# An attention block with two feed-forward halves on one core: split-format key norms, and values made ahead in the odd head's steps

## The reference

```python
qr = q * phase; kr = k * phase                     # rotation, complex
s  = einsum('bihd,bjhd->bhij', qr, conj(kr)).real
qn = (q.real**2 + q.imag**2).sum(-1)               # query norms
kn = (k.real**2 + k.imag**2).sum(-1)               # key norms
maha   = maximum(qn + E*E*kn - 2*E*s, 0) / V       # E, V: per head and distance
logits = coef * log1p(maha / nu) - 0.5 * DH * log(V)
A   = softmax(causal(logits))
out = A @ v;  y = concat(out.real, out.imag) @ Wo
```

## Time and profile before

| | |
|---|---|
| median of 3 runs | 1696.93 us |
| span of the profiled execution | 1693.8 us |
| median less that span | 3.1 us |
| first scores of the loop | 257.64 us into the span |
| TensorE, DVE, ACT, POOL busy | 97%, 88%, 86%, 58% |

### The profile page before, as it was taken

The page is one execution under the profiler, slowest core; times in us unless marked ns, Lnnn a source line. Parts: engine busy times, 40 slices in busy tenths (PEclk is TensorE's granted clock), DMA queues, the critical chain, the costliest instruction groups (busy, mean ns, idle before and its releaser), DMA issues. The chain is left out here.

```text
span 1693.8 us, 30993 instructions
## 1 busy us (share of the span) xinstructions
PE 1642.7 (97%) x9690; PEld 1337.0 (79%) x9690; DVE 1483.9 (88%) x3380; ACT 1452.4 (86%) x2909; POOL 974.3 (58%) x826
## 2 busy tenths in 40 slices
PE   5999988999999999999999999999999999899998
PEld 4787866888888888888788888888887887777876
DVE  6878877999899989999999998999899989977665
ACT  6677678999999999999999999999999999765765
POOL 3564546566566656665655565566566656345565
PEclk9999999999999999999999999999999999999999
DMA  6000032232223322232232323232332222100000
GB/s 177 1 1 1 1 103 66 63 91 62 77 70 75 74 68 79 63 78 65 77 79 63 91 57 82 54 91 60 82 79 63 69 70 51 26 7 7 13 11 15
DMA packets 50482, 100.03 MB, mean 59 GB/s; under 512 B 8208, under 2 KB 25872, under 8 KB 50320
## 3 DMA queue, kind: packets, MB, share of 16 engines
q1 hardware_dynamic: 50320, 98.07, 22.5%
HBM read 17.95 MB, written 5.24 MB: 14 GB/s over the span
## 5 line engine op out<-in xcount | busy, mean ns | idle before, releaser
L1495 POOL TENSOR_TENSOR early<-early 128x1024 f32<-128x1024 f32 x127 | 303.2, 2387 | 470.0 <-PE pS L1183 258.6
L654 POOL TENSOR_TENSOR hid_lo_d<-hid_d,hid_hi_d 128x512 fp32r<-128x512 f32 x176 | 231.5, 1316 | 218.7 <-ACT hid_hi_d L559 212.1
L1387 ACT ACTIVATE early<-early,qnorm 128x128 f32<-128x128 f32 (+3 forms) x512 | 247.0, 554 | 68.3 <-DVE early L1578 66.4
L1183 PE MATMUL pS<-early 128*128 128x128 f32 (+3 forms) x1024 | 297.6, 433 | 0.3 <-PEq L105 0.3
L1371 ACT ACTIVATE early<-early,nmax 128x128 f32<-128x128 f32 (+3 forms) x512 | 281.6, 562 | 6.9 <-DVE nmax L1565 6.7
L1183 PEld LDWEIGHTS pS<-early 128*128 128x128 f32 x1024 | 164.7, 191 | 96.0 <-issue 61.4
L1574 DVE SCALAR_TENSOR_TENSOR pS<-pS,ek 128x1280 f32<-128x1280 f32 x128 | 191.4, 1495 | 55.3 <-PE pS L1183 54.4
L1504 POOL TENSOR_TENSOR ek<-early 128x128 f32<-128x128 f32 (+3 forms) x256 | 216.7, 881 | 3.6 <-ACT early L1379 3.0
L1504 POOL TENSOR_TENSOR ek<-decay,early 128x128 f32<-128x128 f32 (+3 forms) x256 | 215.3, 876 | 0.0
L1400 ACT ACTIVATE early<-early,params 128x512 f32<-128x512 f32 (+1 forms) x256 | 196.9, 819 | 0.0
L1198 PEld LDWEIGHTS pV<-ones,early 128*128 128x128 f32 x1016 | 134.3, 193 | 61.3 <-issue 61.3
(11 more groups left out here) (394 smaller groups left out, 3883.7 us busy)
## 6 DMA issues: line engine op xcount, KB each, us to landing
early<-early SPq DMA_DIRECT2D x263, 256.0 KB, 3.6
early<-trig_d SPq DMA_DIRECT2D x64, 64.0 KB, 2.0
trig_d<-early SPq DMA_DIRECT2D x3, 1024.0 KB, 6.9
early<-in_w SPq DMA_DIRECT2D x3, 704.0 KB, 9.0
x_sb<-in_x SPq DMA_DIRECT2D x4, 512.0 KB, 8.4
early<-in_wqk SPq DMA_DIRECT2D x16, 128.0 KB, 3.4
cos<-trig_d SPq DMA_DIRECT2D x32, 64.0 KB, 2.3
sin<-trig_d SPq DMA_DIRECT2D x32, 64.0 KB, 2.1
```

What stands on the lines that cost most here:

```text
L654: g.tensor_tensor(hid_lo[:, par], hid[:, par], hid_hi[:, par].bitcast(F32), ALU.subtract).then_inc(lo_done, 1)
L1183: last = pe.matmul(s.pS[:, span(I)], rot[:, I * P:(I + 1) * P], rot[:, N:N + (I + 1) * P], start=True, stop=True)
L1387: last = a.activation(u[:, span(I)], u[:, span(I)], ACT.Relu, bias=qnorm[:, r % 2, I:I + 1])
L1495: g.tensor_tensor(rot[:], by_cos[:], crossed[:], ALU.add).then_inc(S["rot_done"], 1)
```

## The change

Key norms. GpSimd (POOL) makes a high and a low half of the squared keys, ahead of `rotate` in each step. TensorE takes the four query-norm products first, waits for both halves, and makes the key norms as two split products with a copy of the ones in F32R. ACT may overwrite the squares when the low half is made.

Values. The batches of a pair get other steps: batches 0, 1, 2 of the next pair are made in steps 11, 13, 15 of this pair (odd head), batches 3 to 7 in steps 1, 3, 5, 7, 8 of their own pair. The first pair keeps its batches in steps 0 to 7, and the last has none in its odd head. There are four buffers for even-head values in place of three, and the waits count values as they are made.

Room in SBUF comes from a smaller scratch for dynamic DMAs.

```diff
+                step(v.memset(s.ones[:], 1.0))
+                v.tensor_copy(s.ones_r[:], s.ones[:]).then_inc(s.S["ones_done"], 1)
...
+        sq_hi, sq_lo = (sb(f"sq_{half}", [P, N], F32R) for half in ("hi", "lo"))
...
-        val_even = [sb(f"val_even{k}", [P, N]) for k in range(3)]
+        val_even = [sb(f"val_even{k}", [P, N]) for k in range(4)]
...
+        EARLY, LATER = {11: 0, 13: 1, 15: 2}, {1: 3, 3: 4, 5: 5, 7: 6, 8: 7}
+
+        def value_at(n):
+
+            i, r = n // STEPS, n % STEPS
+            if i == 0 and 0 <= r < B:
+                return r
+            if 0 < i < H // 2 and r in LATER:
+                return i * B + LATER[r]
+            if 0 <= i < H // 2 - 1 and r in EARLY:
+                return (i + 1) * B + EARLY[r]
+            return None
...
             # norms, TensorE
-                if live(i, r - 2) and parity(r - 2) == 0:
-                    wait(pe, S["val_done"], values_made(i, r - 2))
-                pe.matmul(s.p6[:], s.ones[:], squares[:, N:2 * N], start=True, stop=True).then_inc(S["kn_done"], 1)
+                wait(pe, S["val_done"], values_before(n - 1))
                 for I in range(TILES):
                     last = pe.matmul(s.p5[:, I:I + 1], squares[:, I * P:(I + 1) * P], s.ones[:, 0:1],
                                      start=True, stop=True)
                 last.then_inc(S["q2_done"], 1)
+                pe.wait_ge(S["ones_done"], 1)
+                pe.wait_ge(S["sq_hi"], n)
+                pe.wait_ge(S["sq_lo"], n)
+                pe.matmul(s.p6[:], s.ones_r[:], sq_lo[:], start=True, stop=False)
+                pe.matmul(s.p6[:], s.ones_r[:], sq_hi[:], start=False, stop=True).then_inc(S["kn_done"], 1)
...
-                wait(pe, S["val_done"], values_made(i, r))
-                val = val_even[r % B % 3] if parity(r) == 0 else val_odd[r % B]
+                wait(pe, S["val_done"], values_needed(n))
+                val = val_even[r % B % 4] if parity(r) == 0 else val_odd[r % B]
...
-                if live(i, r) and parity(r) == 0:
-                    values(i, r)
+                if live(i, r) and value_at(n) is not None:
+                    values(i, r, value_at(n))
...
             # square, ACT
                 wait(a, S["q2_done"], n)
+                wait(a, S["sq_lo"], n - 1)
                 a.activation(squares[:], s.pQK[:], ACT.Square).then_inc(S["sq_done"], 1)
...
-                if live(i, r) and parity(r) == 0:
-                    values_out(i, r)
+                if live(i, r) and value_at(n) is not None:
+                    values_out(value_at(n))
...
+            def split(i, r):
+                n = i * 16 + r
+                g.wait_ge(S["sq_done"], n + 1)
+                g.wait_ge(S["kn_done"], n)
+                g.tensor_copy(sq_hi[:], squares[:, N:2 * N]).then_inc(S["sq_hi"], 1)
+                g.wait_ge(S["sq_hi"], n)
+                g.tensor_tensor(sq_lo[:], squares[:, N:2 * N], sq_hi[:].bitcast(F32), ALU.subtract).then_inc(S["sq_lo"], 1)
...
                     if (i, r) != (0, -1):
+                        split(i, r + 1)
                         rotate(i, r + 1)
                     spread(i, r + 1)
...
-    nc = bacc.Bacc("TRN2", target_bir_lowering=False, num_devices=1)
+    nc = bacc.Bacc("TRN2", target_bir_lowering=False, num_devices=1, dynamic_dma_scratch_size=1024)
```

More of the change, by code:

```diff
@@ L884, in _ @@
             if first:
-                v.memset(s.ones[:], 1.0)
+                step(v.memset(s.ones[:], 1.0))
+                v.tensor_copy(s.ones_r[:], s.ones[:]).then_inc(s.S["ones_done"], 1)
                 v.memset(half_pi[:], float(np.pi / 2))
@@ L1106, in parity, with values_before, values_needed @@
             return (r // B) % 2
-        def values_made(i, r):
-            return i * B + (r // 16) * B + (r % B + 1 if parity(r) == 0 else B)
+        EARLY, LATER = {11: 0, 13: 1, 15: 2}, {1: 3, 3: 4, 5: 5, 7: 6, 8: 7}
[8 more added lines that the diff above has]
+            return None
+        def values_before(n):
+            return sum(value_at(m) is not None for m in range(n))
+        def values_needed(n):
+            return n // STEPS * B + n % B + 1
         FRONT, EXP, HALF, LOW, SQUARE, LN, MASK = (1, 2), (2, 3), (3, 6), (4, 7), (3, 5), (4, 6), (6, 7)
@@ L1229, in turn, with values @@
                 last.then_inc(S["tr_done"], 1)
-            def values(i, r):
-                b = r % B
+            def values(i, r, k):
+                pair_, b = k // B, k % B
                 if live(i, r + 1):
@@ L1235, in values @@
                     wait(pe, S["norm_done"], i * 16 + r + 2)
-                wo = tuple(w[:, bass.ds((i * 2 + r // B) * P, 2 * P)] for w in s.wp)
+                wo = tuple(w[:, pair_ * 2 * P:(pair_ + 1) * 2 * P] for w in s.wp)
                 for J in range(TILES):
@@ L1405, in square, with values_out @@
                 wait(a, S["q2_done"], n)
+                wait(a, S["sq_lo"], n - 1)
                 a.activation(squares[:], s.pQK[:], ACT.Square).then_inc(S["sq_done"], 1)
[L1408 to L1412, removed]
+            def values_out(k):
+                pair_, b = k // B, k % B
+                a.wait_ge(S["v_done"], k + 1)
+                wait(a, S["av_done"], (pair_ if b > 3 else pair_ - 1) * STEPS + (b - 4) % B + 1)
+                wait(a, S["av_done"], (pair_ - 1) * STEPS + B + b + 1)
+                for h, val in enumerate((val_even[b % 4], val_odd[b])):
                     last = a.activation(val[:].rearrange("p (j d) -> p j d", j=TILES),
@@ L1792, in program @@
         s.ones = sb("ones", [P, P])
+        s.ones_r = sb("ones_r", [P, P], F32R)
         s.dist = sb("dist", [P, SW])
@@ L1816, in program @@
         names = ("w_in trig_in0 trig_in1 w_hi w_lo hp_done arg_done decay_done decay2_done lnv_done lam0_done "
-                 "lam_done qk_done bs_done crossed_in cos_done sq_done rot_done norm_done q2_done qn_done kn_done "
+                 "lam_done qk_done bs_done crossed_in cos_done sq_done ones_done sq_hi sq_lo rot_done norm_done q2_done qn_done kn_done "
                  "ek_done s_done w_done t_done relu_done ln_done zred_done exp_done v_done "
```

## The result

The changed kernel takes 1753.05 us (median of 4 runs, 1749.02 to 1756.85), the kernel before 1697.2 in the same comparison: 1.0328 times as long, 95% interval 1.0315 to 1.0341. The span of the profiled execution is 1752.4, 58.6 more than before. The first scores start at the same place (257.59 us, before 257.64); the last step's scores start 59.6 later, and what follows takes 1.0 less. So all of it lies in the 128 steps.

A forecast was written before the change was run, and what follows sets the result against it. TensorE issues without a gap, but the DVE and ACT loop is as long, and bank pS nearly so. First head pair 3, six middle 39, last 6: + 48 on the median 1696.9, so 1745; range 1690 to 1795.

The forecast's parts named there:

- V step: A step of the 128-step loop that also makes values; 10.05 us in the kernel before.
- N step: A step of the loop without values; 8.70 us in the kernel before.
- The pair: An N step and the V step behind it: + 0.45 from the longer square-to-key-norms path, + 0.65 with the port.
- The port: POOL and DVE's peaks (L1565) exclude each other on SBUF; POOL's subtraction waits for the last piece, 0.2 per pair.
- Steps 8, 9 and 10: Middle head pairs: step 8, V behind V, - 0.15; steps 9 and 10, N behind N, + 0.4 for step 10.
- Builds: ACT's builds for a next head, ahead of the square, lengthen steps 2, 4 and 6: 1.64 per head pair.
- the sign that I gave for hidden builds: If pairs are right and steps 2, 4 and 6 aren't longer than 10 and 12, the builds were hidden.
- The sum of a middle head pair: 4.8 for pairs and steps 8 to 10, plus 1.64 for builds: 6.4 us, 39 for six.
- First and last head pair: Ends of the loop, where values lie in other steps than in middle head pairs: about 3 and 6 us more.
- The rival in which the port decides: Split and peaks exclude each other piece by piece: 1.4 per pair in place of 0.65; 1784 us, chance 0.16.
- what I named as signs: TensorE idle before key norms in V steps behind N, pairs 19.2 to 19.5, longer L1565, POOL near 80%, TensorE under 95%.

The follow-up runs named there:

- the kernel with the high half only: Changed kernel without the low half: POOL's subtraction and TensorE's low product left out, so key norms are rounded; 1707.34 us, 1.0061 times the kernel before.

## Why the prediction was right, and where it was not

The time (1745 forecast, 1753 measured) and the cause were right: the split doesn't fit between square and key norms in a V step behind an N step. That the number came so near is in part luck: two terms of the middle head pairs were off, and they nearly cancel. By head pairs: the first + 11.4 (forecast 3), six middle ones + 41.0 (39), the last + 7.1 (6).

- *The pair.* Forecast + 0.65, measured + 0.24 (18.99). The copy took 0.61 where I took 0.78; POOL began 0.07 after the square (1022.33 + 1.01 = 1023.34 to 1023.41) where I took 0.17 from a start that waited for TensorE; the key norms began 0.14 after the subtraction where I took 0.05. By the Trainium skill, GPSIMD Engine Reference, "Elementwise — side-by-side cycle accounting", the estimate for the copy was 0.44: the measured value lies between it and the row of L1488.
- *The port.* I had POOL's subtraction wait for the last piece, 0.2 on the path. It was the other way: POOL goes on, and DVE's last piece takes 0.4 more. That isn't added to the wait; it is a second path of the same length. Over the whole trace 115 pieces of the peaks took 49 us more than their free durations (0.35, 0.62, 0.75 and 0.49 by size); before, 16 pieces 5 us. Which of the two loses hangs on hundredths of a microsecond. Over the traces of all kernels with a copy, the 153 pieces that started with it or up to 0.042 before it took 0.40 to 0.45 longer; the 50 that started 0.046 to 0.2 before it kept their time, and the copy took 0.83 to 1.15. The Trainium skill (SBUF — State Buffer, "Who interferes with whom") says that issue order decides who blocks. By the starts in the profile that holds only with this margin: the piece at 1023.40 is 0.01 ahead of the copy at 1023.41, and it is the piece that takes longer. It ends 0.27 after the copy, and takes 0.48 alone, so by these rows part of its work was done while the copy ran.
- *Steps 8, 9 and 10.* V behind V 9.86 (forecast - 0.15, measured - 0.18); N behind N 9.11 (+ 0.4, + 0.41). The size was right, the reason only half: the kernel with the high half only has 9.11 as well, without TensorE's wait.
- *Builds.* 10.94, 11.12 and 11.18 where the clock held, against 10.48: 1.80 per head pair; forecast 1.64. They lengthen the V steps 3, 5 and 7, not the N steps 2, 4 and 6, which are 8.50 like 12 and 14. So the sign that I gave for hidden builds (2, 4 and 6 no longer than 10 and 12) came although the builds cost their price: the sign was wrong, not the term.
- *The clock.* Not in my sum, and not among the rivals. In twelve of the middle steps, eleven of them steps 3, 5 and 7, it fell after waits of 1.18 us and more between query norms and key norms (1.06 idle by the profile's bracket in the step shown); these steps are about 1.6 longer than their like: 19 us, 3.2 per head pair. Seven waits of that length in the middle head pairs were not followed by a fall, and none of the plain waits of 0.82 (0.70 in the bracket) was.
- *The sum of a middle head pair.* 7 x 0.24, + 0.60 for step 10 (9.11 for the 8.51 of other N steps), - 0.18 for step 8, - 0.18 for step 9 (8.50 for 8.68), + 1.80, + 3.2, + 0.44 for the two steps 8 of 11.18, - 0.63 for steps of the kernel before that were longer than their like: 6.7 of the 6.8 measured. The forecast had 6.4, with 2.9 too much for the pairs and nothing for the clock.
- *First and last head pair.* Three values now lie in the first head pair and not in the last, 3 x 1.35 = 4 us of the one for the other; I had left that out, and in the sum it cancels. Beyond that, step 0 of the first took 11.64 for 8.27 (TensorE waits 2.74 for the low half, and its clock falls), and step 8 of the first (13.46 for 8.62) and step 14 of the last (15.63 for 11.22) each hold a piece of the peaks stretched by 2.1, nearly the length of a rotate (2.40), and a half-clock stretch beside it. The rival in which the port decides had this mechanism; it came in single steps, not in every pair.

Of what I named as signs: the wait in V steps behind N (0.82 and 1.2) and none in N steps behind V came, TensorE is at 94%, L1598 is longer; pairs are 18.99, not 19.2 to 19.5, and POOL is at 70%, not 80%.

What stays open: why some waits of 1.18 are followed by a fall of the clock and others, as in step 5 of the pair shown (11.12), are not. Length alone doesn't decide it: in the last head pair waits of 1.39 and 1.47 (in the bracket) were not followed by one. It wasn't tried.

## What to carry to other kernels

A step that fills all engines has more than one chain of its own length: before an edit shortens one engine's work, lay out every hand-over that the edit lengthens, and the one behind it. Here 0.37 us less on TensorE was paid with 2 us of POOL in a place that had 0.58. When a change adds work on POOL, look which DVE operations with two SBUF inputs run at that time; and when it adds a wait to TensorE, reckon with a lower clock behind it, and try to fill the wait if it can't be avoided.

## What the runs showed of the hardware that was not expected

- TensorE's granted clock fell from 2.4 to 1.2 GHz inside a loop in which it was over 90% busy, after single waits of little more than 1 us (12 of 19 in the middle head pairs). With 0.7 us of unread products in the wait it did not fall in those steps, and five such products per V step behind N made another kernel 40 us faster.
- DVE operations that meet a run of POOL operations can lose to each of them in turn: three pieces of 0.62, 0.75 and 0.48 us took 1.04, 1.75 and 2.60. Whether the first one loses turned on whether it began less or more than about 0.044 us before POOL's copy.
- A POOL copy of 128x512 from float32 to the split format took 0.61 us where no piece of the peaks was in its way, the subtraction 1.33.
